# Cross-attention with image tokens: inputs given transposed, one PSUM bank for preparation and output, score transposes two heads ahead

## What is computed

```python
q = heads(x @ W_q); k_t = heads(text @ W_k); v_t = heads(text @ W_v)
probs_t = softmax(q @ k_t^T * 16**-0.5)                  # 112 x 371 for each head
text_out = probs_t @ v_t
k_ip, v_ip = heads(ip @ W_k_ip), heads(ip @ W_v_ip)      # ip: the last 4 context rows
attn_scores = q @ k_ip^T * 16**-0.5                      # the image scores, 112 x 4
qsem = l2norm(probs_t @ text)
fused = attn_scores + 0.5 * qsem @ l2norm(ip)^T
probs_ip = softmax(fused) * spatial_mask[None, None, :, None]
out = (text_out + probs_ip @ v_ip) @ W_out + b_out + x
```

## Time and profile before

| | |
|---|---|
| median of 3 runs (lowest, highest) | 840.43 us (840.39, 840.55) |
| the profiled execution | 839.78 us |
| its span, first to last instruction | 838.1 us |
| TensorE busy | 798.9 us, 95% |
| VectorE, ScalarE, GpSimd busy | 82%, 67%, 48% |

### The profile page before, as it was taken

How to read it: one execution, slowest core, us unless ns; L and a number is a source line. 1 busy time by engine, 2 the same in 40 slices (tenths; PEclk the granted TensorE clock), 3 DMA queues, 4 the chain that set the end, 5 groups by cost and what they waited for, 6 DMA issues and landing times.

```text
span 838.1 us, 24219 instructions
## 1 busy us (share of the span) xinstructions
PE 798.9 (95%) x8294; PEld 626.5 (75%) x8294; DVE 685.0 (82%) x2003; ACT 563.0 (67%) x1366; POOL 405.9 (48%) x516
## 2 busy tenths in 40 slices
PE   3989999999999999999999999999999999999983
PEld 2667778787787878778787877878787787877662
DVE  3777888887888888788888878888887888878893
ACT  2366767776677777667777766777776677767660
POOL 4123463645546364554536455453645545364652
PEclk9999999999999999999999999999999999999996
DMA  7322221121212112121211212121121212011000
GB/s 202 95 71 68 62 63 50 50 81 43 67 42 61 52 51 80 43 66 44 63 50 50 81 42 74 37 63 50 51 80 42 73 39 62 14 47 40 8 2 14
DMA packets 62947, 47.62 MB, mean 57 GB/s; under 512 B 10314, under 2 KB 56762, under 8 KB 62826
## 3 DMA queue, kind: packets, MB, share of 16 engines
q1 hardware_dynamic: 59898, 42.71, 19.3%
q10 hardware_dynamic: 2928, 3.36, 1.4%
HBM read 18.38 MB, written 2.38 MB: 25 GB/s over the span
## 4 chain that ended last, share of the span: by engine, by line
PE 92%; DVE 2%; issue 2%; DMA 1%; ACT 1%; POOL 1%; POOLq 0%; SPq 0%; DVEq 0%; ACTq 0%
PE ps_prep L438 18%; PE ps_gram L553 18%; PE ps_pT L535 14%; PE ps_gram L554 11%; PE ps_score L527 6%; PE ps_prep L511 5%; PE ps_light L438 3%; PE ps_light L460 2%; PE ps_val L561 2%; PE ps_val L563 2%; DMA ctx_sb<-in_ctx 1%; PE ps_light L586 1%; PE ps_prep L507 1%; PE ps_prep L489 1%; PE ps_prep L491 1%
## 5 line engine op out<-in xcount | busy, mean ns | idle before, releaser
L373 POOL TENSOR_TENSOR dual<-prob 112x371 f32<-112x371 f32 x320 | 277.9, 868 | 391.0 <-ACT prob L737 369.2
L553 PE MATMUL ps_gram<-gram_hi,pT_hi 125*128 125x371 f16 (+1 forms) x960 | 303.9, 320 | 0.0
L731 ACT ACTIVATE pT_hi<-ps_pT 125x336 f16<-125x336 f32 x320 | 145.4, 454 | 165.3 <-PE ps_pT L535 157.6
L554 PE MATMUL ps_gram<-gram_lo,pT_hi 125*128 125x371 f16 (+2 forms) x960 | 255.9, 267 | 0.0
L891 DVE TENSOR_REDUCE low<-ps_score 112x1 f32<-112x371 f32 x320 | 172.6, 540 | 66.8 <-PE ps_score L527 64.4
L724 ACT ACTIVATE prob<-ps_score,low 112x371 f32<-112x371 f32 x320 | 184.1, 576 | 59.9 <-DVE low L891 59.3
L896 DVE TENSOR_TENSOR pT_lo<-ps_pT,pT_hi 125x336 f16<-125x336 f32 x320 | 160.5, 502 | 31.7 <-ACT pT_hi L731 26.1
L906 DVE CUSTOM_DVE_ANT_0 quad_junk<-ps_gram,dual 112x371 f32<-112x371 f32 x320 | 170.5, 533 | 4.7 <-POOL dual L373 1.8
L535 PE MATMUL ps_pT<-ident,prob 112*125 112x112 f32 x960 | 160.4, 275 | 7.8 <-DVE pT_lo L896 2.6
L561 PE MATMUL ps_val<-val,pT_hi 125*128 125x42 f16 (+1 forms) x960 | 166.9, 182 | 0.0
L535 PEld LDWEIGHTS ps_pT<-ident,prob 112*125 112x125 f32 x960 | 140.2, 188 | 35.4 <-issue 22.2
(11 more groups left out here) (198 smaller groups left out, 1444.6 us busy)
## 6 DMA issues: line engine op xcount, KB each, us to landing
ctx_sb<-in_ctx SPq DMA_DIRECT2D x15, 750.0 KB
k_st<-k_hi SPq DMA_DIRECT2D x64, 70.3 KB, 2.1
k_st<-k_lo SPq DMA_DIRECT2D x62, 70.3 KB, 2.1
q_st<-q_hi SPq DMA_DIRECT2D x64, 48.0 KB, 1.9
k_st<-k_hi SPq DMA_DIRECT2D x64, 46.9 KB, 2.0
k_st<-k_lo SPq DMA_DIRECT2D x62, 46.9 KB, 2.0
q_st<-q_lo SPq DMA_DIRECT2D x60, 48.0 KB, 2.0
x_sb<-in_x SPq DMA_DIRECT2D x16, 140.0 KB, 2.2
```

Source lines behind the costliest of these rows:

```text
L373: nc.gpsimd.tensor_tensor(dual[:, h % 2, :], prob[:, h % 4, 0:TX], prob_16[:, h % 2, :], ALU.subtract).then_inc(s_dual, 1)
L553: nc.tensor.matmul(ps_gram[h % 2][:, 0:TX], hi, gh[0:TROWS[i], i, :], start=(i == 0), stop=False, skip_group_check=True)
L554: last = nc.tensor.matmul(ps_gram[h % 2][:, i * TC:TX], hi, gl[0:TROWS[i], i, i * TC:TX], start=False, stop=(i == NT - 1), skip_group_chec ...
```

## The change

The host hands over x and the context transposed (and the image rows once more by themselves), so `turn` is gone from TensorE: ScalarE and VectorE split the loaded tiles straight from SBUF, in five pieces per batch instead of four, and three of the five low halves go to GpSimd. The image scores are four more columns of the score matmul, and ScalarE copies these four columns out for each head. The bank `ps_light` is given up: its place is taken by a second bank for the transposed probabilities, and the four `finish` stages now write into `ps_prep`, in steps 13, 15, 17 and 19 (the last batch: 18 instead of 19). Each `make` waits for the `finish` stages before it, and each `finish` for the pieces before it. Scores are made four heads ahead and transposes two heads ahead. The eviction of the last `finish` stage stands in VectorE's step 0 of the next body. The multiplication of the image probabilities by the mask is merged with the one before it. Residual and store move too.

```diff
-TURN_STEP = {1: 0, 3: 1, 5: 2, 11: 3}
+SPLIT_STEP = {5: 0, 7: 1, 9: 2, 12: 3, 14: 4}
+POOL_PIECES = (2, 3, PIECE_X)
...
-FINISH_STEP = {13: 0, 15: 1, 17: 2, 18: 3}
+FINISH_STEP = {13: 0, 15: 1, 17: 2, 19: 3}
+STORE_STEP = 1
+LAST_FINISH_STEP = {13: 0, 15: 1, 17: 2, 18: 3}
...
+SCORES_AHEAD, TURNS_AHEAD = 4, 2
+PROBS, TURNED = 6, 3
...
-        ps_pT = ps("ps_pT", [P, 512])
+        ps_pT = [ps(f"ps_pT{i}", [P, 512]) for i in range(2)]
...
-        ps_light = ps("ps_light", [P, 512])
...
-            def make(a, k, banks=(ps_prep,)):
+            def make(a, k, banks=(ps_prep,), at=0):
...
                 reached(pe, s_prep_lo, NM * a.n + k + 1 - len(banks))
+                reached(pe, s_fin_ev, NF * (a.n - 2) + sum(step < at for step in FINISH_STEP))
...
                 reached(pe, s_prob, g - 1)
-                nc.tensor.matmul(ps_score[h % 2][:, 0:TX], q_st[b.odd][:, h // 2, h % 2, :], k_st[b.odd][:, h // 2, 0:TX],
+                reached(pe, s_ip_score, g - 1)
+                nc.tensor.matmul(ps_score[h % 2][:, 0:T], q_st[b.odd][:, h // 2, h % 2, :], k_st[b.odd][:, h // 2, :],
                                  start=True, stop=True).then_inc(s_score, 1)
...
-                reached(pe, s_pT_lo, g)
+                reached(pe, s_pT_lo, g - 1)
...
-                nc.tensor.matmul(ps_val[:, OW + hh * NIP:OW + (hh + 1) * NIP], q_st[b.odd][:, h // 2, h % 2, :],
-                                 k_st[b.odd][:, h // 2, TX:T], start=True, stop=True, skip_group_check=True).then_inc(s_val, 1)
-
-            def finish(f, k):
-
+
+            def finish(f, k, made):
+
+                pe.wait_ge(s_prep_lo, made)
+                reached(pe, s_fin_ev, NF * f.n + k)
                 if k == 0:
                     pe.wait_ge(s_soft, SOFT * (f.n + 1))
-                    last = nc.tensor.transpose(ps_light[0:H * NIP, 0:S], fprob[:, :, :].rearrange("s h n -> s (h n)"), ident[0:S, 0:S])
+                    last = nc.tensor.transpose(ps_prep[0:H * NIP, 0:S], fprob[:, :, :].rearrange("s h n -> s (h n)"), ident[0:S, 0:S])
...
                     if prepare and h in MAKE_STEP:
-                        make(b.next(), MAKE_STEP[h])
-                    if turning and h in TURN_STEP:
-                        light_bank_free(turned, finished)
-                        turn(b.next().next(), TURN_STEP[h])
-                        turned = turned + 1
-                    if finishing and h in FINISH_STEP:
-                        light_bank_free(turned, finished)
-                        finish(b.last(), FINISH_STEP[h])
-                        finished = finished + 1
+                        make(b.next(), MAKE_STEP[h], at=h)
+                    if finishing and h in finish_step:
+                        finish(b.last(), finish_step[h], NM * (b.n + 1) + (sum(step < h for step in MAKE_STEP) if prepare else 0))
...
+                if h == 0:
+                    reached(act, s_soft, SOFT * (b.n - 2) + SOFT_ARGS)
+                nc.scalar.activation(ip_score[b.odd][:, h, :], ps_score[h % 2][0:S, TX:T], ACT.Copy).then_inc(s_ip_score, 1)
...
-                elif k == 12:
-                    last = v.tensor_scalar(fmax[:, 1, :], fmax[:, 2, :], mask_sb[:, 0:1], None, ALU.mult)
                 else:
                     reached(dve, s_fin, NF * f.n)
-                    last = pair(fprob[:, :, :], fexp[:, :, :], over_ip(fmax[:, 1, :]), ALU.mult)
+                    last = v.scalar_tensor_tensor(out=fprob[:, :, :], in0=fexp[:, :, :], scalar=mask_sb[:, 0:1], in1=over_ip(fmax[:, 2, :]),
+                                                  op0=ALU.mult, op1=ALU.mult)
...
+                    if h == 0 and b.n >= 2:
+                        finish(b.last().last(), NF - 1)
```

More of the change, by code:

```diff
@@ L28 @@
 OW = HH * 2 * VW
-HALF_W = OW + HH * NIP
 EPS = 1e-12
@@ L148, in build @@
         val = [sb(f"val{i}", [TC, NT, H, 2 * VW], F16) for i in range(2)]
[L150 to L153, removed]
+        low = sb("low", [S, PROBS])
+        prob = sb("prob", [S, PROBS, T])
+        pT_hi = sb("pT_hi", [TC, TURNED, NT, S_PAD], F16)
+        pT_lo = sb("pT_lo", [TC, TURNED, NT, S_PAD], F16)
         prob_16 = sb("prob_16", [S, 2, TX], F16)
@@ L420, in body @@
                         batch_k_ip(b.next())
-                    if prepare and h == RESIDUAL_STEP:
-                        residual(b.next())
+                    if h == RESIDUAL_STEP:
+                        residual(b)
+                    if turning and SPLIT_STEP.get(h - 1) in POOL_PIECES:
+                        split_lo(b.next().next(), SPLIT_STEP[h - 1])
             def tail(b):
@@ L610, in _ @@
                 make(start, k, SETUP_BANKS)
-            pe.wait_ge(s_setup_ev, 1)
+            pe.wait_ge(s_ip, 32)
             pe.wait_ge(s_w[2], 16)
-            light_bank_free(NX, 0)
             for j in range(CC):
                 for e in range(EC):
-                    last = nc.tensor.matmul(ps_light[0:channels(j), j * 64:(j + 1) * 64], w_raw[:, e, 2, j * P:j * P + channels(j)],
+                    last = nc.tensor.matmul(ps_pT[1][0:channels(j), j * 64:(j + 1) * 64], w_raw[:, e, 2, j * P:j * P + channels(j)],
                                             ip_T[:, e, :], start=(e == 0), stop=(e == EC - 1))
             last.then_inc(s_setup_pe, 1)
-            pe.wait_ge(s_setup_ev, 3)
-            for k in range(NX):
-                turn(second, k, TURN_BANKS)
             pe.wait_ge(s_const, 3)
@@ L632, in _ @@
             pe.wait_ge(s_ipdiag, 1)
-            light_bank_free(2 * NX, 0)
-            nc.tensor.matmul(ps_light[0:S, 0:64], ones[:, :], ip_diag[:, :], start=True, stop=True).then_inc(s_setup_pe, 1)
+            pe.wait_ge(s_setup_ev, 2)
+            nc.tensor.matmul(ps_pT[1][0:S, 0:64], ones[:, :], ip_diag[:, :], start=True, stop=True).then_inc(s_setup_pe, 1)
             scores(start, 0)
@@ L769, in _ @@
             for k in range(NX):
-                turn_hi(start, k, TURN_BANKS)
+                split_hi(start, k, first=True)
             split_weight(wq_hi[:, :, :], wq_sb[:, :, :], s_wq, 2)
@@ L813, in body @@
                         fin_exp(b.last())
-                    if finishing and h == H - 1:
+                    if not prepare and h == H - 1:
                         store(b.last())
@@ L953, in soft @@
                 elif k == 7:
[L954 to L956 removed]
+                    dve.wait_ge(s_ip_score, H * (f.n + 1))
+                    last = pair(fused[:, :, :], fused[:, :, :], ip_score[f.odd][:, :, :], ALU.subtract)
                 elif k == 8:
```

298 lines of the change are left out of this document (151 added, 147 removed).

## The result

The change makes the kernel slower: 899.29 us (898.87 to 900.15) against 840.41 us (839.50 to 840.55), a ratio of 1.0704 (95% interval 1.0686 to 1.0723).

A forecast was written before the change was run, and what follows sets the result against it. TensorE's list bounds bodies 1 to 14: 45.5 us plus 8.5 of waits is 54.0. Setup 46.6, body 0 44.9, bodies 1 to 14 755.2, body 15 33.5, end 18.6: span 898.8, time 900 us (884 to 918).

The forecast's parts named there:

- The bound and TensorE's list: Bodies 1 to 14: TensorE's own list is the bound and falls from 48.8 to 45.5 us a body.
- rival of the falling clock: Steps 13 to 0: granted 1.2 GHz there, work doubles, some 11 us a body, about 1,050 us; chance 4%.
- The hand-overs: Steps 13 to 19, 0 and 2: TensorE waits for late evictions, mainly of ps_prep, 8.5 us a body.
- none stands ahead of an eviction: ScalarE's 20 image-score copies a body, 0.1 us each (at most 0.32), delay no eviction.
- replace evictions of like size: ScalarE's splits of the loaded tiles take the place of similar evictions, so no cost was counted.
- Setup: Before body 0: loses 15 transposes of the second batch, -1.5 us (0 to -4), from 48.1 to 46.6.
- Little before them, where loads arrive: Setup, ahead of the second batch's 15 transposes (1.7 us): little time is saved there.
- Body 15: Last body: VectorE is the limit, 34.2 less the mask multiply, so 33.5 us, from 39.3.
- Body 0: First body, without finish: 48.2 less 1.72, 0.47 and 1.4 idle, plus 0.4 for Q, 44.9 us.
- bodies 1 to 14: Middle bodies: 14 x 54.0 us, less 0.8 as body 1 has no finish before it, 755.2 us.
- the end: Chain after body 15: 19.3 less 0.7, 18.6 us.
- The costs put at nothing: ScalarE's copies, GpSimd's subtractions (2.6 us a body) and VectorE's port waits (up to 2.6) leave the sum unchanged.

The follow-up runs named there:

- E3: Changed kernel with only ScalarE evicting ps_prep ahead of the transposes, VectorE's order as in the change: 907.41 us, 1.0811 of the kernel before.
- E6: E1 with the pieces in another order, all of G before V: 829.78 us, 0.9881 of the kernel before.
- E12: Kernel before the change with finish stages 0, 1 and 2 moved into ps_prep, all else unchanged: 924.23 us, 1.0995 of the kernel before.
- E2: Changed kernel with the finish stages in a bank of their own, one ps_pT and the shorter leads: 828.97 us, 0.9871 of the kernel before.
- E1: Changed kernel with ScalarE and VectorE both evicting ps_prep ahead of the transposes instead of behind: 814.34 us, 0.9696 of the kernel before.
- E8: E1 with GpSimd's four powers in body 15 replaced by copies, leaving out batch 14's inverse root: 813.40 us, 0.9680 of the kernel before.
- E9: E1 with pieces G and V in turn (V0, G0, V1, G1, G2, V2): 805.35 us, 0.9582 of the kernel before.
- E4: Changed kernel with GpSimd's three subtractions done on VectorE: 901.59 us, 1.0731 of the kernel before.
- E5: E1 with GpSimd's three subtractions done on VectorE: 831.69 us, 0.9907 of the kernel before.

## Why the prediction was right, and where it was off

**The bound and TensorE's list: right.** 45.5 us a body were forecast. Measured: 53.95 less the waits of 8.3 that the next two points list (7.9 and 0.4) is 45.7. The granted clock was 1.00 in all bodies, so the rival of the falling clock did not come, but E3 and E6 show how near it was.

**The hand-overs: right, nearly term by term.** Forecast and measured (distance of starts less 0.025), in steps 13 to 19, 0 and 2, the waits ahead of what follows G0, stage 0, G1, stage 1, G2, stage 2, V2, stage 3 and Q:

| | 13 | 14 | 15 | 16 | 17 | 18 | 19 | 0 | 2 | sum |
|---|---|---|---|---|---|---|---|---|---|---|
| forecast | 1.68 | 0.57 | 1.41 | 0.81 | 1.23 | 0.81 | 0.79 | 0.81 | 0.37 | 8.5 |
| measured | 1.67 | 0.57 | 1.24 | 0.74 | 1.14 | 0.81 | 0.70 | 0.74 | 0.28 | 7.9 |

A wait worked out from offsets read where nobody waits held to 0.17 us where someone does. In G0's two errors cancel: its eviction ended 3.03 us after the step's start, not 2.95, and TensorE went on 0.06 after it, not 0.15. Sharing the bank is shown as the cause from both sides: put alone into the kernel before it costs 84 us (E12, three of the four stages), and taken out of the kernel after it gives 70, although the second `ps_pT` and the longer lead go with it (E2). Three quarters of its price hang on the evictions standing behind those of the transposes: with the same bank and the order turned, 2.1 of the 7.9 us a body are left, and E1 is 85 us faster than the change.

**What was not forecast: a wait in step 10.** TensorE waits there for ScalarE to copy `ps_val` out:

```profile
436.52 0.21 PE L560 MATMUL ps_gram<-gram_lo,pT_hi 121*128 121x121 f16 x1
436.93 0.19 PE L567 MATMUL ps_val<-val,pT_hi 125*128 125x42 f16 x1 [0.20 <-ACT half_sb L745]
```

It costs 0.4 us a body (0.41 between the two, 0.05 where nothing waits). The copy stands behind a split, an exponential and the copy of image scores in ScalarE's step 9. The prediction had said of the copies that "none stands ahead of an eviction", which is wrong here, but the split is what costs: body 14 has the same copies and no splits, its step 10 takes 3.05 us instead of 3.42, and the wait is gone. The splits "replace evictions of like size", the prediction said, and did not ask in which step they stand. With 7.9 for 8.5 it evened out: a body of 53.95 where 54.0 stood. That is luck.

**Setup: a term mis-sized.** -1.5 us was forecast (0 to -4), -5.1 measured. "Little before them, where loads arrive" failed. First matmul of Q, in the kernel before and then after:

```profile
18.56 0.27 PE L438 MATMUL ps_prep<-x_hi,wq_hi 128*128 128x112 f16 x1 [2.09 <-DVE wq_lo L829]
```

```profile
12.67 0.25 PE L466 MATMUL ps_prep<-x_hi,wq_hi 128*128 128x112 f16 x1 [12.67 <-DVE wq_lo L835]
```

It starts 5.9 us earlier. Both wait last for VectorE's low half of the weights, and before the change the evictions of turns, which wait for TensorE, stood ahead of it in ScalarE's and VectorE's lists. ScalarE began the high half of `wq` at 15.96 us, right behind the last of them, and now begins it at 10.04. That is read from the code and the two traces; no run here isolates it.

**Body 15: a term mis-sized.** 33.5 forecast, 35.1 measured. I took VectorE's busy time for the limit; it is busy 30.7 of 35.1. E8 shows that GpSimd's powers hold four steps, worth 1.5 us there. Body 0 (44.9 forecast, where its own terms add up to 45.0; 45.8 measured), bodies 1 to 14 (755.2, 754.5) and the end (18.6, 18.8) are within a microsecond. Setup's -3.6 is set off in part by the +1.6 of body 15 and the +0.9 of body 0. The mechanism was right; that the sum, 898.8 us for a span of 897.2, came closer than its parts is luck.

**The costs put at nothing: right.** ScalarE's copy of four columns takes 0.18 us, 57.5 in all, between my bounds; E1, E2 and E9 have it and are faster than before. GpSimd's subtractions take 0.877 us; moving them back gives nothing (E4) or costs (E5). The merged multiply, two instructions made one, takes 0.79 us on average. The multiply and GpSimd in E1, then in E9, body 5 of both:

```profile
308.86 0.90 POOL L399 TENSOR_TENSOR dual<-prob 112x371 f32<-112x371 f32 x1
```

```profile
307.88 0.36 DVE L971 SCALAR_TENSOR_TENSOR fprob<-fexp,mask_sb,fmax 112x80 f32<-112x80 f32 x1
307.25 0.89 POOL L399 TENSOR_TENSOR dual<-prob 112x371 f32<-112x371 f32 x1 [0.55 <-ACT prob L738]
```

In E1 the multiply begins at 308.96 and ends at 309.85, 0.09 us after GpSimd's subtraction; in E9 it begins at 307.88 and ends at 308.24, 0.10 after it. So it is in every body of every kernel with this instruction; in the last batch, where GpSimd does nothing beside it, it takes 0.30 us. What it costs above 0.30 is a wait for the instruction that GpSimd is in. In "SBUF — State Buffer", section "Who interferes with whom", the Trainium skill has a VectorE instruction with two SBUF inputs contend with one of GpSimd that reads SBUF; these traces agree. The two splits on VectorE took 0.55 us on average, so they seldom had long to wait; the one of 1.25 us in E5 ran beside GpSimd's subtraction for 0.85 of it. As long as TensorE is not held by VectorE this costs nothing.

## What to carry to other kernels

A bank of PSUM given to a second user costs what the first one's eviction is late, and that can be read before the change: the end of each eviction, counted from the start of the step in which the bank will be wanted, less what TensorE has to do until then. If the sum is large, look first at what stands ahead of the eviction in the evicting engines' lists: here the same shared bank was 7% slower with the evictions second and 3% faster with them first. Both engines of a two-step eviction have to be turned: VectorE's order alone gave a quarter of the gain, ScalarE's alone nothing in a body.

## What the runs showed of the hardware

- TensorE stood idle once in a body for 1.73 to 1.79 us in E3 (bodies 1 to 13) and for 1.82 to 1.89 us in E6. In five bodies of each the granted clock then fell, to 0.55 over 2.7 us in E3 and to 0.51 over 2.9 us in E6 (+1.03 and +1.6 us a body), and in the other bodies it stayed at 1.00. The length of the idle time alone does not decide it: E3 has bodies with 1.79 us of both kinds, and in E6 the five ahead of a fall were 1.82 us, the other nine 1.88 or 1.89. With idle times of up to 1.6 us (after, E12) no body showed it. The Trainium skill, "TensorE: Matmul & The Clock Gate", section "A second HAM failure mode: psum-queue depth-cycling", says that a kernel which waits often and briefly for PSUM is throttled on and off; nine such waits a body, of 0.3 to 1.7 us by starts, did not do it in the kernel after.
- A VectorE multiply of 112 x 80 with two SBUF inputs takes 0.30 us alone; beside a GpSimd subtraction it ended 0.09 to 0.10 us after that one, whenever it had begun (in most bodies it took 0.36 us in E9, 0.67 in E5, 0.88 or 0.89 in E1).
- A power of 112 x 5 on GpSimd takes 1.17 to 1.25 us on average, a copy of as many elements 0.19, a subtraction of 112 x 371 0.87.
- ScalarE's copy of 112 x 4 out of PSUM takes 0.18 us (0.16 to 0.22), a third of the 0.57 of an exponential of 371 columns.
